# Spreading a tile's epilogue over the next tile's first passes, and moving the staging and its transposes later, in an eight-core LayerNorm, attention and ternary FFN kernel

## What is computed

```
qkv = einsum('bsd,fd->bsf', x, w_qkv)          # one head
attention = softmax(q k^T * SCALE, axis=1)     # axis 1 is the head axis, of length 1
values = attention @ v ;  out = values @ w_o.T
absmean(W) = sign(W/g) * min(round(|W/g|), 1),  g = mean(|W|) + 1e-6
h = gelu(x @ absmean(W_fc).T)                  # 1024 -> 4096, exact gelu
h = layernorm(h) * ln_w + ln_b
y = h @ absmean(W_proj).T                      # 4096 -> 1024
```

## Time and profile before

| | |
|---|---|
| time, median of 2 runs | 3674.81 us (3673.48 to 3676.15) |
| profiled execution: time, span of its slowest core | 3694.57 us, 3693.0 us |
| spans of cores 0 to 3; of 4 to 7 | 3681.4 to 3693.0; 3661.0 to 3666.5 us |
| busy PE, DVE, ACT, POOL | 2922.8, 2239.3, 868.3, 80.5 us |
| start of the first fc matmul | 646.43 us |

### The profile page before, as it was taken

One profiled execution on the slowest core, in us unless ns is written; L12 is line 12 of the kernel. 1 busy time (PEld: TensorE's weight loads), 2 busy tenths in 40 slices (PEclk: granted clock), 3 DMA queues, 4 the chain that ended last, 5 costly groups with the idle time before them and its releaser, 6 DMA issues.

```text
span 3693.0 us, 66863 instructions; the slowest of 8 cores (3661.0 to 3693.0 us)
## 1 busy us (share of the span) xinstructions
PE 2922.8 (79%) x22170; PEld 1968.6 (53%) x22170; DVE 2239.3 (61%) x5462; ACT 868.3 (24%) x2133; POOL 80.5 (2%) x164
## 2 busy tenths in 40 slices
PE   0002242998989898989898989898989898989896
PEld 0002140665656565656565656565656565656564
DVE  5667775656565656565656565656565666655444
ACT  1114301222222222222222222222222222221211
POOL 0000202000000000000000000000000000000000
PEclk9999999999999999999999999999999999988898
DMA  4438541000000000000000000000000000000000
GB/s 148 123 123 258 182 133 59 12 7 18 7 14 11 12 13 12 13 12 13 13 13 12 13 13 13 12 13 13 13 13 13 13 13 13 13 13 1 12 1 12
DMA packets 38403, 130.26 MB, mean 35 GB/s; under 512 B 7216, under 2 KB 7344, under 8 KB 38064
## 3 DMA queue, kind: packets, MB, share of 16 engines
q1 hardware_dynamic: 16560, 58.83, 5.0%
q10 hardware_dynamic: 9216, 33.56, 2.9%
q0 software_dynamic: 12288, 33.59, 2.6%
HBM read 109.15 MB, written 16.78 MB: 34 GB/s over the span
## 4 chain that ended last, share of the span: by engine, by line
PE 72%; DVE 13%; DMA 4%; DVEq 4%; issue 3%; ACT 3%; POOL 1%; ACTq 1%; SPq 0%; POOLq 0%
PE proj_ps L229 36%; PE fc_ps L692 34%; DVE cols L51 4%; DVEq L50 4%; DMA xs<-wfcT 4%; DVE x1s L51 3%; DVE bnp L51 1%; PE trp_ps L673 1%; ACT ATT L51 1%; DVE gps_t L51 1%; DVE l2t_t L51 1%; DVE V L51 1%; DVE rrq L51 1%; POOL l2t_t L369 1%; ACTq L50 1%
## 5 line engine op out<-in xcount | busy, mean ns | idle before, releaser
L229 PE MATMUL proj_ps<-qp_t,gps_t 128*128 128x512 bf16 x6144 | 1447.2, 386 | 171.6 <-DVE gps_t L51 171.5
L692 PE MATMUL fc_ps<-l2t_t,qf_t 128*128 128x256 bf16 x12288 | 1457.7, 277 | 0.7 <-ACT l2t_t L51 0.7
L692 PEld LDWEIGHTS fc_ps<-l2t_t,qf_t 128*128 128x128 bf16 x12288 | 1205.7, 99 | 186.1 <-issue 4.0
L229 PEld LDWEIGHTS proj_ps<-qp_t,gps_t 128*128 128x128 bf16 x6144 | 607.0, 99 | 821.6 <-issue 248.0
L51 DVE TENSOR_TENSOR S<-S,g 128x256 f32<-128x256 f32 x496 | 211.0, 426 | 786.6 <-ACT g L51 783.5
L51 ACT ACTIVATE g<-fc_ps 128x256 f32<-128x256 f32 x512 | 196.2, 383 | 2055.5 <-PE fc_ps L692 1905.9
L51 DVE SCALAR_TENSOR_TENSOR rrq<-g,lnw_c,gps_t 128x256 f32<-128x256 f32 x512 | 248.4, 485 | 38.8 <-issue 0.6
L51 ACT ACTIVATE l2t_t<-trp_ps 128x128 bf16<-128x128 f32 x768 | 212.8, 277 | 133.5 <-PE trp_ps L673 73.5
L51 DVE TENSOR_TENSOR gps_t<-rrq,gps_t 128x256 bf16<-128x256 f32 x512 | 217.5, 425 | 40.8 <-issue 3.5
L51 DVE TENSOR_TENSOR S<-S,gsq 128x256 f32<-128x256 f32 x496 | 211.0, 425 | 42.2 <-issue 6.1
L51 ACT ACTIVATE gsq<-g 128x256 f32<-128x256 f32 x512 | 213.3, 417 | 43.2 <-issue 1.8
(11 more groups left out here) (128 smaller groups left out, 1384.6 us busy)
## 6 DMA issues: line engine op xcount, KB each, us to landing
x1s<-wpT ACTq DMA_DIRECT2D x64, 512.0 KB, 4.1
xs<-x SPq DMA_DIRECT2D x64, 512.0 KB, 3.7
xs<-wfcT SPq DMA_DIRECT2D x48, 512.0 KB, 5.5
out<-x1s POOLq DMA_DIRECT2D x32, 512.0 KB, 2.9
xs<-wfcT POOLq DMA_DIRECT2D x16, 512.0 KB, 3.8
x1s<-wvT POOLq DMA_DIRECT2D x8, 512.0 KB, 7.8
x1s<-woT POOLq DMA_DIRECT2D x8, 512.0 KB, 6.8
l2t_t<-gps_t POOLq DMA_DIRECT2D x96, 0.2 KB, 1.5
```

The source lines that it names most:

```text
L229: last = tensor.matmul(out=proj_ps[tg][:, 512 * hh:512 * hh + 512], lhsT=gps[jj % 2][s][:, 128 * tg:128 * tg + 128], rhs=qp[jj][:, 512 * h ...
L692: last = tensor.matmul(out=fc_ps[j % 2][:], lhsT=qf[d][:, 128 * j:128 * j + 128], rhs=l2t[i % 2][s][d][:], start=(s == 0 and d == 0), stop ...
```

## The change

Three things are moved, and one queue is changed. No arithmetic is added or removed.

1. The epilogue of tile i-1 is cut into six pieces, which DVE does behind passes 0 to 5 of tile i (before: all of it ahead of pass 0). Pieces 0 and 1 read `proj_ps0` and `proj_ps1` and count `sv_psr`.
2. The preparation of the next tile comes later: x1 of group 0 behind pass 6, its statistics behind 7, group 1 behind 8 and 9, apply behind 10 and 11, and the staging blocks behind 12 to 27 (before: 7 to 22). ACT takes the two square roots behind passes 8 and 10, each between two table loads of its own. The transposes begin in pass 12 (before: 10), their evacuations in pass 13 (before: 11); eight transposes instead of four are left for the end of the tile.
3. All 32 loads of the quantizing loop are issued by SP.

```diff
+        def emit_epi_piece(vector, ii, piece):
+            if piece == 0:
+                vector.wait_ge(ss_r3, ii + 1)
+                vector.wait_ge(st_projj, 32 * (ii + 1))
...
+                vector.scalar_tensor_tensor(out=x1s[gr0 % 4][:], in0=proj_ps[0][:],
...
+                vector.inc(sv_psr, 1)
+            elif piece == 1:
+                vector.scalar_tensor_tensor(out=x1s[gr1 % 4][:], in0=proj_ps[1][:],
...
+                vector.inc(sv_psr, 1)
...
-            for t in range(0, 32, 2):
+            for t in range(32):
...
-                sync.dma_start(out=xs[0][:], in_=src).then_inc(B_x2s[0], 16)
+                sync.dma_start(out=xs[t % 2][:], in_=src).then_inc(B_x2s[t % 2], 16)
...
-                for t in range(1, 32, 2):
...
-                    gpsimd.dma_start(out=xs[1][:], in_=srcq).then_inc(B_x2s[1], 16)
...
-                        if j == 4 and i + 1 <= nt - 1:
+                        if j in (8, 10) and i + 1 <= nt - 1:
...
-                        if i + 1 <= nt - 1 and 11 <= j <= 31:
-                            emit_group_evac(scalar, i + 1, 2 * (j - 11))
+                        if i + 1 <= nt - 1 and 13 <= j <= 31:
+                            emit_group_evac(scalar, i + 1, 2 * (j - 13))
...
-                    if i + 1 <= nt - 1 and 10 <= j <= 31:
-                        emit_group_T(tensor, i + 1, 2 * (j - 10))
+                    if i + 1 <= nt - 1 and 12 <= j <= 31:
+                        emit_group_T(tensor, i + 1, 2 * (j - 12))
...
-                    for ql in range(44, 48):
+                    for ql in range(40, 48):
...
-                if i >= 1:
-                    emit_epilogue(vector, i - 1)
                 for j in range(32):
...
+                    if i >= 1 and j <= 5:
+                        emit_epi_piece(vector, i - 1, j)
...
-                        elif 7 <= j <= 22:
-                            emit_stage_block(vector, i + 1, j - 7)
+                        elif 12 <= j <= 27:
+                            emit_stage_block(vector, i + 1, j - 12)
```

More of the change, by code:

```diff
@@ L235, in emit_proj @@
             last.then_inc(st_projj, 1)
+        def emit_epi_piece(vector, ii, piece):
+            tg = piece // 3 if piece >= 2 else piece
+            gr0, gr1 = 2 * ii, 2 * ii + 1
+            if piece == 0:
+                vector.wait_ge(ss_r3, ii + 1)
+                vector.wait_ge(st_projj, 32 * (ii + 1))
+                for tg_ in range(2):
+                    vector.tensor_scalar(out=nmrc[tg_][:], in0=m3c[tg_][:],
+                                         scalar1=r3c[tg_][:], scalar2=-2.0,
+                                         op0=OP.mult, op1=OP.mult)
+                vector.scalar_tensor_tensor(out=x1s[gr0 % 4][:], in0=proj_ps[0][:],
+                                            scalar=r3c[0][:], in1=x1s[gr0 % 4][:],
+                                            op0=OP.mult, op1=OP.add)
+                vector.inc(sv_psr, 1)
+            elif piece == 1:
+                vector.scalar_tensor_tensor(out=x1s[gr1 % 4][:], in0=proj_ps[1][:],
+                                            scalar=r3c[1][:], in1=x1s[gr1 % 4][:],
+                                            op0=OP.mult, op1=OP.add)
+                vector.inc(sv_psr, 1)
+            elif piece in (2, 4):
+                tg_ = 0 if piece == 2 else 1
+                gr = 2 * ii + tg_
+                vector.scalar_tensor_tensor(out=x1s[gr % 4][:], in0=U[:],
+                                            scalar=nmrc[tg_][:], in1=x1s[gr % 4][:],
+                                            op0=OP.mult, op1=OP.add)
+            else:
+                tg_ = 0 if piece == 3 else 1
+                gr = 2 * ii + tg_
+                vector.tensor_add(out=x1s[gr % 4][:], in0=x1s[gr % 4][:], in1=V[:])
+                vector.inc(sv_y3, 1)
         def emit_epilogue(vector, ii):
@@ L255, in emit_epilogue, with emit_x1_add, emit_x1_bn @@
                 vector.inc(sv_y3, 1)
+        def emit_x1_add(vector, ip1, tg):
+            gr = 2 * ip1 + tg
+            vector.wait_ge(sm_xs[gr % 2], 16 * (gr // 2 + 1))
+            if gr >= 4:
+                vector.wait_ge(sm_outs[gr % 4], 16 * (gr // 4))
+            vector.tensor_add(out=x1s[gr % 4][:], in0=xs[gr % 2][:],
+                              in1=ATT[gr // 16][:])
+        def emit_x1_bn(vector, ip1, tg):
+            gr = 2 * ip1 + tg
+            vector.bn_stats(out=bnp[:, 0:6], in_=x1s[gr % 4][:, 0:512])
+            vector.bn_stats(out=bnp[:, 6:12], in_=x1s[gr % 4][:, 512:1024])
+            vector.bn_aggr(out=bno2[:, 2 * tg:2 * tg + 2], in_=bnp[:])
+            vector.tensor_scalar_add(out=varc[:], in0=bno2[:, 2 * tg + 1:2 * tg + 2],
+                                     scalar1=EPS)
+            vector.reciprocal(out=rcc[tg][:], in_=varc[:])
+            vector.inc(sv_stat, 1)
         def emit_x1_stats(vector, ip1, only_tg=None):
             for tg in ((0, 1) if only_tg is None else (only_tg,)):
[L259 to L271, removed]
+                emit_x1_add(vector, ip1, tg)
+                emit_x1_bn(vector, ip1, tg)
         def emit_apply(vector, ip1, tg):
@@ L495, in _ @@
                         scalar.inc(ss_gsq, 1)
-                        if j == 4 and i + 1 <= nt - 1:
+                        if j in (8, 10) and i + 1 <= nt - 1:
+                            tg = 0 if j == 8 else 1
                             scalar.preload_act_table(AF.Sqrt)
[L498 to L502, removed]
+                            scalar.wait_ge(sv_stat, 2 * (i + 1) + tg + 1)
+                            scalar.activation(out=r2c[tg][:], in_=rcc[tg][:],
+                                              func=AF.Sqrt)
+                            scalar.inc(ss_r2, 1)
                             scalar.preload_act_table(AF.Gelu)
-                        if i + 1 <= nt - 1 and 11 <= j <= 31:
-                            emit_group_evac(scalar, i + 1, 2 * (j - 11))
-                            emit_group_evac(scalar, i + 1, 2 * (j - 11) + 1)
+                        if i + 1 <= nt - 1 and 13 <= j <= 31:
+                            emit_group_evac(scalar, i + 1, 2 * (j - 13))
+                            emit_group_evac(scalar, i + 1, 2 * (j - 13) + 1)
                     if i + 1 <= nt - 1:
-                        for q in range(42, 48):
+                        for q in range(38, 48):
                             emit_group_evac(scalar, i + 1, q)
```

23 lines of the change are left out of this document (11 added, 12 removed).

## The result

The changed kernel takes 3809.61 us (median of 11 runs), the kernel before in the same series 3675.26 us (10 runs). Over undisturbed runs the ratio is 1.0359, 95% interval 1.0335 to 1.0384. The kernel is slower, by 134 us between the medians. The forecast was slower by 80 us, 3755, in a range of 3738 to 3795. The direction was right; the size was not, and the time lies outside the range.

What follows compares the result with a forecast made beforehand. PE was taken to set the pace of the passes and to stop only at tile boundaries. Terms 78 + 22.5 - 3 - 12 - 6 = 79.5, say +80 us on the median, gave 3755 us, range 3738 to 3795.

Steps and rivals of the forecast that it cites:

- waits in passes 12 and 13: PE waits twice a tile for blocks DVE stages in the same pass, 2.6 us each, 78 us in all.
- slower clock behind them: No term in the sum; matmuls behind the new waits of passes 12 and 13 were counted at full speed.
- eight transposes at the end: At a tile's end, four more evacuations on ACT lengthen the boundary by 1.5 us, +22.5 us in all.
- four transposes fewer in the passes: Two passes a tile lose their transposes ahead of fc, -0.2 us a tile, -3 us in all.
- epilogue in pieces: At the boundary the first projection starts 0.8 us earlier, behind pass 1 and piece 1 on DVE; -12 us in all.
- slower first projection: No term in the sum; before the change, the first projection behind the boundary was read at 4.63 us instead of 2.75.
- quantizing loop: In the prologue, all loads from SP save the 0.5 us ahead of POOL's issue; -6 us, bounds -8 to 0.
- The failed step: In passes 12 and 13, each new wait was priced at its 2.6 us alone, without a clock fall behind it.
- the clock falls in the new waits: Rival: in passes 12 and 13 the granted clock falls, 1.9 us a fall, 3783 or 3811 us; chance 0.14.
- The forecast's own sign of being wrong: Granted clock under 1.0 in passes 12 to 15, one of three signs named as showing the forecast wrong.
- two-falls time: The clock rival with two falls in each tile, +56 us, 3811 us; the rival's chance as a whole 0.14.
- both small gains at their better bounds: Range's lower end, 3738 us: epilogue at -1.1 us a boundary, quantizing loop at -8 us, with waits at 2.43 us.

## Why the prediction was wrong, point by point

| term, for 15 tiles | forecast | measured |
|---|---|---|
| waits in passes 12 and 13 | +78 | +77 idle, +85 from projection to next fc |
| slower clock behind them | 0 | +47 |
| eight transposes at the end | +22 | +23 |
| four transposes fewer in the passes | -3 | -3 |
| epilogue in pieces | -12 | -11 |
| slower first projection | 0 | +7 |
| quantizing loop | -6 | -7 |
| sum | +80 | about +141 |

- *The waits: right*, in place, number and length. Idle time is 2.56 us in the mean. Counted between starts a little more goes: projection to next fc is 5.64 and 5.43 us (1297.16 to 1302.80, 1307.08 to 1312.51) where rows 4 have 2.70 (1267.59 to 1270.29), so 2.94 and 2.73 us, 85 us for 15 tiles.
- *The failed step*: the sum put the matmuls behind the new waits at full speed, a cost of 0, and left the fall to the rival "the clock falls in the new waits", which I gave 0.14. It came in 28 of 30 cases, at 1.6 us each instead of the 1.9 of its price: 45 us in the fc groups, and some 2 more in the projections behind the second ones (2.87 us instead of 2.75 in the rows above). The argument against it was that 2.6 us is shorter than the gaps with a fall in rows 8, and that there is full work between. Neither counted: between full passes the rows of before only had gaps of 1 us without and of 10 us with a fall, and nothing between, so they bounded the cost from both sides and gave no ground for the lower one. The sum took zero; the bounds had been 0 and 56. The forecast's own sign of being wrong, a granted clock under 1.0 in passes 12 to 15, is what the profile shows. That the rival's two-falls time, 3811, is within 1.4 us of the measured one is in part luck: it had 9 us too much for the falls, and nothing for the slower first projection.
- The Trainium skill (TensorE: Matmul & The Clock Gate, HAM oscillation) says that a kernel that waits between bursts of matmuls has its clock halved each time; the waits of its example are some 3 to 5 us. The trace agrees in kind, with 28 slow fc groups of 4.38 us in the mean, and shows it behind waits of 2.5 to 2.9 us.
- *The range* left the case out: 3795 stood for falls in about half the waits, while the rival's own end was 3811. It does not follow from the forecast's own prices either: falls in half the waits give 3783, and both small gains at their better bounds with waits of 2.43 us give 3743, not 3738.
- *The epilogue: right.* 9.61 us against 10.35 in the mean is -0.7 us, by the mechanism named: the second read behind all of pass 1 decides. The runs with both reads together show it.
- *The transposes at the end: right.* The four more cost 1.55 us in evacuations; from last projection to gelu it is 15.01 us against 13.47 in the mean, 1.54 in all.
- *The first projection* was taken as unchanged; it takes 4.79 us in the mean instead of 4.33. The run with the transposes alone shows the same, 4.84. Why it is slower is open.
- *The loop: right*, and tested alone: -6.6 us. The estimate from the Trainium skill (DMA: Bandwidth & Descriptors, Latency and other measured facts), -12, was not borne out.
- *A tile* was forecast to be 5.9 us longer; the terms of the sum give 5.7 (85.5 us in 15 tiles). It is 10.0 us longer, 197.85 us against 187.87, the latter without the tile of before that lies in the slower-clock stretch.
- *141 and 134.* The sum is counted on profiles, and the tiles agree with it: 15 times 10.0 us, less the loop's 7, is 143. In the profile before, all four cores of the one die had stretches at a granted clock of 0.81, for core 3 that of rows 8; against the spans of the other die, 3661 to 3666.5, the profile after is 143 to 148 us longer. In the profile after no core has such a stretch. The kernel before took 3669.8 to 3674.8 us on the chips of the experiments, 135 to 140 less than the changed kernel. How much of the 7 us between sum and medians is due to such stretches in the runs behind the 3675.26 us was not shown.

## What to carry to other kernels

When a step is moved, move its consumer by as much: here the producer went five passes later and the consumer two, and one pass more saved 122 us. Price a new wait on TensorE at its length plus what the clock takes behind it, and, where the profile shows gaps on both sides of its length, keep both prices in the range. To take work off a boundary, ask which instruction there releases the waiting engine, and move everything but that.

## What the runs showed of the hardware that I had not expected

- An idle time of 2.5 to 2.9 us of TensorE amid full passes is followed by a lower granted clock in 28 of 30 cases (in another kernel 15 of 15); one of 1.4 to 1.9 us in 3 of 30, the three longest; one of 0.3 to 0.7 us in none of 30. The record of the clock reads 1.00 during the idle time and falls to 0.50 behind it, 0.4 to 1.4 us into the work in 27 of 28 cases, so the cost stands in the matmuls behind the wait and not in the row of the wait.
- Matmuls that compute nothing of use made two kernels faster: 48 us for 600 of them in the waits, 37 us for 660 at the boundaries.
- A slow first projection covered that VectorE was late for the next pass. Made fast at ten of 15 boundaries, it exposed a wait of 1.00 us there, and 4 us were left of the 24 expected.
